# Moving the second expert bias from VectorE into the matmul of a gated attention and expert kernel

## The reference

```
x = x + tanh(g_xattn) * attention(layernorm(x), ctx, bias)     # 16 heads of 16, q/k/v with LoRA terms
x = x + tanh(g_ffn)   * ffn(layernorm(x))

def ffn(x):                       # 16384 tokens, E = 8 experts, H = I = 256
    idx = argmax(softmax(x @ Wg + bg))
    h = gelu(x @ W1[e] + b1[e])
    y = h @ W2[e] + b2[e]         # b2 is E x 256
    return y of expert idx of each token
```

## Time and profile before

| what | value |
|---|---|
| median of 3 runs | 1362.39 us (1362.06 to 1363.53) |
| profiled execution | 1363.53 us |
| its span, first to last instruction | 1361.7 us |
| TensorE busy | 1318.7 us, 97% of the span |
| VectorE busy | 1094.0 us, 80% |
| GpSimd busy | 1039.8 us, 76% |
| ScalarE busy | 889.3 us, 65% |
| granted TensorE clock, mean | 0.982 of 2.4 GHz |
| moved by DMA | 265.05 MB, mean 195 GB/s |

### The profile page before, as it was taken

How to read it: one execution, slowest core, us unless ns; L and a number is a source line. 1 busy time by engine, 2 the same in 40 slices (tenths; PEclk the granted TensorE clock), 3 DMA queues, 4 the chain that set the end, 5 groups by cost and what they waited for, 6 DMA issues and landing times.

```text
span 1361.7 us, 43106 instructions
## 1 busy us (share of the span) xinstructions
PE 1318.7 (97%) x13172; PEld 1137.3 (84%) x13172; DVE 1094.0 (80%) x2484; ACT 889.3 (65%) x1912; POOL 1039.8 (76%) x1186
## 2 busy tenths in 40 slices
PE   8999999999999999999999999999996599999997
PEld 6888888888888888888888888888885488888886
DVE  4898899899989898998998999989897355555555
ACT  3777777777777777777777777777775233333332
POOL 3778888888888888888888888888887254555445
PEclk7999999999999999999999999999999699999999
DMA  7656666666666666666666666666651598889984
GB/s 223 189 158 181 172 193 186 174 185 193 172 180 191 182 173 180 196 176 177 190 187 172 189 189 174 179 191 184 171 165 45 175 279 280 285 282 280 284 272 132
DMA packets 350200, 265.05 MB, mean 195 GB/s; under 512 B 17673, under 2 KB 313022, under 8 KB 350016
## 3 DMA queue, kind: packets, MB, share of 16 engines
q1 hardware_dynamic: 336656, 228.89, 59.4%
q0 software_dynamic: 12960, 34.63, 6.8%
q10 hardware_dynamic: 528, 0.84, 0.2%
HBM read 227.17 MB, written 38.94 MB: 195 GB/s over the span
## 4 chain that ended last, share of the span: by engine, by line
PE 92%; DVE 3%; issue 1%; DMA 1%; ACT 1%; POOL 1%; SPq 0%; POOLq 0%; DVEq 0%; ACTq 0%
PE bank L481 17%; PE bank L490 16%; PE bank L466 10%; PE bank L631 9%; PE bank L644 9%; PE bank L520 9%; PE bank L570 8%; PE bank L535 4%; PE bank L620 2%; PE bank L581 2%; PE bank L592 2%; PE bank L595 2%; PE bank L511 1%; DVE sc L820 1%; DVE negmax L826 1%
## 5 line engine op out<-in xcount | busy, mean ns | idle before, releaser
L378 POOL TENSOR_TENSOR sc<-sc,negmax 128x1024 f32<-128x1024 f32 x256 | 482.6, 1899 | 49.6 <-DVE negmax L826 45.7
L820 DVE TENSOR_TENSOR sc<-bank,sc 128x512 f32<-128x512 f32 x512 | 328.5, 683 | 44.6 <-PE bank L466 44.6
L826 DVE TENSOR_REDUCE negmax<-sc 128x8 f32<-128x1024 f32 x256 | 312.4, 1220 | 16.9
L694 ACT ACTIVATE PT<-bank 128x512 f32<-128x512 f32 x512 | 279.3, 606 | 0.2
L481 PE MATMUL bank<-cst,sc 128*128 128x128 f32 x2048 | 273.1, 276 | 0.0
L435 POOL DMA_INDIRECT out<-og,ids x142 | 139.8, 984 | 151.9 <-issue 130.8
L481 PEld LDWEIGHTS bank<-cst,sc 128*128 128x128 f32 x2048 | 226.1, 141 | 25.7 <-issue 25.5
L708 ACT COPY OT<-bank 128x512 f32<-128x512 f32 x128 | 75.0, 586 | 151.6 <-PE bank L520 151.6
L421 POOL DMA_INDIRECT rows_dram<-x2n,slot_i x128 | 138.6, 1083 | 29.5 <-issue 26.2
L466 PE MATMUL bank<-KT,QT 32*128 32x256 f32 x2048 | 146.6, 400 | 2.3 <-issue 1.8
L985 DVE SCALAR_TENSOR_TENSOR og<-bank,tg,sc 128x512 f32<-128x512 f32 x71 | 53.3, 751 | 109.7 <-PE bank L644 77.3
(11 more groups left out here) (114 smaller groups left out, 2186.2 us busy)
## 6 DMA issues: line engine op xcount, KB each, us to landing
sc<-in_bias SPq DMA_DIRECT2D x256, 512.0 KB
xg<-rows_dram SPq DMA_DIRECT2D x71, 272.0 KB
w_sb<-in_w SPq DMA_DIRECT2D x71, 257.0 KB
sc<-in_w SPq DMA_DIRECT2D x71, 256.0 KB
x_sb<-in_x SPq DMA_DIRECT2D x128, 128.0 KB, 2.1
ctx_sb<-in_ctx_in SPq DMA_DIRECT2D x128, 128.0 KB, 4.9
rows_dram<-vacant SPq DMA_DIRECT2D x9, 272.0 KB, 5.6
out<-og,ids POOLq DMA_INDIRECT x142
```

Source lines behind the costliest of these rows:

```text
L378: nc.gpsimd.tensor_tensor(s, s, m, ALU.add).then_inc(sub_ok, 1)
L694: nc.scalar.activation(PT[:, t.slot(2), 512 * q:512 * q + 512], b_t[q % 2][:], ACT.Exp).then_inc(pt_ready, 1)
L820: nc.vector.tensor_tensor(s, b_s[q][:], s, ALU.add).then_inc(s_used, 1)
L826: nc.vector.tensor_reduce(negmax[:, t.slot(2), 8 * h:8 * h + 8], sc[:, t.slot(4), 1024 * h:1024 * h + 1024].rearrange("p (h k) -> p h k", ...
```

## The change

The bias b2 is now added on TensorE. At the start VectorE splits b2 (8 x 256 float32) into three bf16 parts whose sum is b2; they are written to a small tensor in DRAM. In the expert stage SyncE loads the three rows of a tile's expert into partitions 0 to 2 of `b2_sb` (four slots, the other partitions are zero), as a third DMA beside the weights, and Y begins in each half with a matmul of `top3` (ones in partitions 0 to 2, zero elsewhere) and these rows. VectorE's L975, L1005 and L1007 go, as does the broadcast of b2. TILES becomes 72, and the writes of vacant rows are no longer spread over the stage: all eight are issued in the steps 0 to 7 that are written out, and the loads of rows in the loop wait for all of them.

```diff
-TILES = 71
+TILES = 72
+        b2_dram = nc.dram_tensor("b2_dram", (EXPERTS, 3, HID), BF16, kind="Internal").ap()
-        FLOOP = (1, TILES // FU)
+        FLOOP = (1, TILES // FU - 1)
-        TAIL_AT, TAIL_BY = 0, 5
 # SyncE, step 2 of the attention stage
-                    sp.dma_start(b2_all[:].rearrange("p e h -> p (e h)"), b2.rearrange("(a e) h -> a (e h)", a=1)
-                                 .partition_broadcast(P)).then_inc(b2_in, 16)
+                    sp.wait_ge(s_b2, 4)
+                    sp.dma_start(b2_dram, b2_parts[:]).then_inc(b2_out, 16)
 # SyncE, set-up loads
+            load(b2_all[:], b2, s_set)
 # SyncE, expert stage
+            sp.wait_ge(b2_out, 16)
             def fstep(i, k):
-                if k == TAIL_BY:
-                    sp.wait_ge(tail_out, i * 16 + 16)
-                    sp.nop(nofuse=True)
                 t = tile(i, k, -3)
                 if t:
                     if t.reached(8):
                         sp.wait_ge(og_ok, t.n(1, -7))
+                        sp.nop(nofuse=True)
+                    if not isinstance(i, int):
+                        sp.wait_ge(tail_out, 16 * EXPERTS)
                         sp.nop(nofuse=True)
...
                     sp.dma_start(w2_sb[:, t.slot(4)], w2[e]).then_inc(w2_in[t.slot(4)], 16)
-                if k == TAIL_AT:
-                    first = sp.value_load(tail_i[0:1, bass.ds(i, 1)], min_val=0, max_val=DUMMY - FT)
+                    sp.dma_start(b2_sb[0:3, t.slot(4)], b2_dram[bass.ds(e, 1)].rearrange("e p h -> (e p) h")
+                                 ).then_inc(w2_in[t.slot(4)], 16)
+                if isinstance(i, int) and 0 <= k < EXPERTS:
+                    first = sp.value_load(tail_i[0:1, k:k + 1], min_val=0, max_val=DUMMY - FT)
                     sp.dma_start(rows_dram[bass.ds(first, FT), :].rearrange("(p a) r -> p (a r)", p=P),
                                  vacant[:]).then_inc(tail_out, 16)
 # GpSimd, ahead of step 0
+            nc.gpsimd.memset(b2_sb[:], 0.0).then_inc(s_setg, 1)
 # TensorE, Y
-                    pe.wait_ge(w2_in[t.slot(4)], t.per(4, 16, 16))
+                    pe.wait_ge(w2_in[t.slot(4)], t.per(4, 32, 32))
                     for a in range(HALVES):
                         y_half = bank[6 + t.slot(2)][:, HID * a:HID * a + HID]
+                        mm(y_half, top3[:], b2_sb[:, t.slot(4), :], start=True, stop=False)
                         for c in range(KC):
                             ins = mm(y_half, hT[:, t.slot(2), c, a * P:a * P + P],
-                                     w2_sb[:, t.slot(4), c * HID:c * HID + HID], start=(c == 0), stop=(c == KC - 1))
+                                     w2_sb[:, t.slot(4), c * HID:c * HID + HID], start=False, stop=(c == KC - 1))
 # VectorE, set-up
+                nc.vector.memset(top3[:], 0.0).then_inc(s_set3, 1)
+                dve.wait_ge(s_set3, 1)
+                nc.vector.memset(top3[0:3, :], 1.0).then_inc(s_set3, 1)
+                nc.vector.tensor_copy(b2_parts[:, 0, :], b2_all[:]).then_inc(s_b2, 1)
+            def split_b2():
+                dve.wait_ge(s_b2, 1)
+                nc.vector.tensor_tensor(b2_rest[:], b2_all[:], b2_parts[:, 0, :], ALU.subtract).then_inc(s_b2, 1)
+                dve.wait_ge(s_b2, 2)
+                nc.vector.tensor_copy(b2_parts[:, 1, :], b2_rest[:]).then_inc(s_b2, 1)
+                dve.wait_ge(s_b2, 3)
+                nc.vector.tensor_tensor(b2_parts[:, 2, :], b2_rest[:], b2_parts[:, 1, :], ALU.subtract).then_inc(s_b2, 1)
 # VectorE, expert stage
-            dve.wait_ge(b2_in, 16)
-            nc.vector.tensor_scalar(b2_all[:], b2_all[:], tg[:, 1:2], None, ALU.mult).then_inc(b2_ok, 1)
-                    e = dve.value_load(tile_e[0:1, bass.ds(t.n(), 1)], min_val=0, max_val=EXPERTS - 1)
-                    dve.wait_ge(x2g_ok, t.n(HALVES, HALVES))
-                    nc.vector.tensor_tensor(x2g[:, t.slot(2)], x2g[:, t.slot(2)],
-                                            b2_all[:, bass.ds(e, 1), :].broadcast_to([P, HALVES, HID]), ALU.add
-                                            ).then_inc(x2b_ok, 1)
```

More of the change, by code:

```diff
@@ L129, in flamingo_block @@
         bv_all = sb("bv_all", [P, HID])
+        top3 = sb("top3", [P, P], BF16)
         bg_all = sb("bg_all", [P, EXPERTS])
@@ L189, in flamingo_block @@
         w1_sb = sb("w1_sb", [P, 4, KC * HID + KC])
-        b2_all = sb("b2_all", [P, EXPERTS, HID])
+        b2_sb = sb("b2_sb", [P, 4, HID], BF16)
+        b2_all, b2_rest = sb("b2_all", [EXPERTS, HID]), sb("b2_rest", [EXPERTS, HID])
+        b2_parts = sb("b2_parts", [EXPERTS, 3, HID], BF16)
         og = sb("og", [P, 2, HALVES, HID])
@@ L207, in flamingo_block @@
         s_cst, s_id, s_b, s_g, s_set, s_warm = (sem(t) for t in ("s_cst", "s_id", "s_b", "s_g", "s_set", "s_warm"))
-        s_bv, b2_in, b2_ok = sem("s_bv"), sem("b2_in"), sem("b2_ok")
+        s_bv, s_b2, b2_out = sem("s_bv"), sem("s_b2"), sem("b2_out")
         vacant_ok, vacant_out, tail_out = sem("vacant_ok"), sem("vacant_out"), sem("tail_out")
         s_setp, s_setd, s_seta, s_setg = sem("s_setp"), sem("s_setd"), sem("s_seta"), sem("s_setg")
-        s_setb, s_setr, s_ones = sem("s_setb"), sem("s_setr"), sem("s_ones")
+        s_set3, s_setb, s_setr, s_ones = sem("s_set3"), sem("s_setb"), sem("s_setr"), sem("s_ones")
         x_in = [sem(f"x_in{i}") for i in range(8)]
@@ L237, in flamingo_block @@
         w2_in = [sem(f"w2_in{i}") for i in range(4)]
-        ids_ok, inv_ok, x2g_ok, x2b_ok = (sem(t) for t in ("ids_ok", "inv_ok", "x2g_ok", "x2b_ok"))
+        ids_ok, inv_ok, x2g_ok = sem("ids_ok"), sem("inv_ok"), sem("x2g_ok")
         xg_in = [sem(f"xg_in{i}") for i in range(8)]
@@ L242, in flamingo_block @@
         og_out = [sem(f"og_out{i}") for i in range(2)]
-        SETUP_DMAS = 3
+        SETUP_DMAS = 4
         FIRST_DMAS = 2
@@ L364, in _ @@
             run_steps(sp, FFIRST, FLAST, FU, FLOOP, fstep)
-            for n, q in enumerate(og_out):
-                sp.wait_ge(q, 16 * HALVES * len(range(n, TILES, 2)))
+            for q in og_out:
+                sp.wait_ge(q, 16 * HALVES * TILES // 2)
         @block.gpsimd
@@ L934, in _ @@
             set_up_routing()
+            split_b2()
             run_steps(dve, 0, LAST, U, LOOP, step, {dve.engine: 0})
@@ L972, in _ @@
                                     ALU.min).then_inc(tab_ok, 1)
-            dve.wait_ge(b2_in, 16)
-            nc.vector.tensor_scalar(b2_all[:], b2_all[:], tg[:, 1:2], None, ALU.mult).then_inc(b2_ok, 1)
-            dve.wait_ge(tab_ok, 1)
             def fstep(i, k):
@@ L983, in fstep @@
                         dve.wait_ge(og_out[t.slot(2)], t.per(2, 16 * HALVES))
-                    dve.wait_ge(x2b_ok, t.n(1, 1))
+                    dve.wait_ge(x2g_ok, t.n(HALVES, HALVES))
                     nc.vector.scalar_tensor_tensor(out=og[:, t.slot(2)].rearrange("p a h -> p (a h)"),
@@ L1002, in fstep @@
                                                 ALU.subtract, ALU.mult).then_inc(x2g_ok, 1)
-                    if not t.reached(1):
-                        dve.wait_ge(b2_ok, 1)
-                    e = dve.value_load(tile_e[0:1, bass.ds(t.n(), 1)], min_val=0, max_val=EXPERTS - 1)
-                    dve.wait_ge(x2g_ok, t.n(HALVES, HALVES))
-                    nc.vector.tensor_tensor(x2g[:, t.slot(2)], x2g[:, t.slot(2)],
-                                            b2_all[:, bass.ds(e, 1), :].broadcast_to([P, HALVES, HID]), ALU.add
-                                            ).then_inc(x2b_ok, 1)
             run_steps(dve, FFIRST, FLAST, FU, FLOOP, fstep)
```

## The result

The change makes the kernel slower: a median of 1393.0 us (1392.3 to 1395.1) against 1362.5, a ratio of 1.0226 with a 95% interval of 1.0208 to 1.0243. The forecast was 1386.2 us with a range up to 1390.5, so the sign was right and the size too small: +30.5 us where +23.8 was forecast. The profiled execution took 1390.15 us (span 1388.2), 2.9 us under the median; it reached its first tile some 3 us earlier than that of before. The stage of the tiles is what is read from it.

A forecast was written before the change was run, and what follows sets the result against it. TensorE was taken to bound the kernel; 1363.5 + 19.6 (bf16 matmuls 15.8, tile 3.9) + 4.2 (wait) = 1387.3 us for a like execution, 1.1 above the median, so the forecast median was 1386.2 us, range 1381 to 1390.5.

The forecast's parts named there:

- What bounds: Expert stage: TensorE has no gap, so anything added there is paid in full and work taken from VectorE gains nothing.
- Rival E: Expert stage: transfers set the pace, the new matmuls hide and the kernel isn't slower, 1361.8 us; chance 0.03.
- Two more matmuls: Each half of Y in the expert stage: one bf16 matmul at 0.109 us, together 15.8 us.
- Rivals C and D: bf16 matmuls: C, 0.193 or 0.216 us each, 1398 to 1402 us, chance 0.10; D, bare weight loads, 1414 us, chance 0.01.
- The 72nd tile: TensorE's loop in the expert stage takes one more whole tile whatever it holds: +3.9 us.
- SyncE's queue, the pace: Expert stage's start: steps with a vacant write take 4.34 us against TensorE's 4.11, hidden by the queue's lead: 0.
- SyncE's queue, the wait: After the last vacant write: TensorE stands still once at T(11) and H(10), +4.2 us (3.3 to 5.2).
- Rival A: Wait for the vacant writes costs nothing, as writes or loads land sooner: 1382.0 us; chance 0.17.
- The clock: TensorE's granted clock after the stall: a fall to half was counted only in rival B, at +2.0 us.
- main case: TensorE's +19.6 us and one stall of +4.2 us: median 1386.2 us, own range 1385 to 1388; chance 0.52.
- rival B: The stall also costs the clock, +2.0 us, 1388.2 us, or is longer through traffic, to 1389.5 us; chance 0.15.
- What hides: VectorE's lost bias addition, splitting b2, fills, the dropped broadcast and the kernel's end: counted 0, at most -0.8 us.

The follow-up runs named there:

- b2_act_nobf16: Changed kernel with vacant writes one in eight tiles, bias loads issued by ScalarE, and no bf16 matmuls (b2 isn't added): 1366.9 us, ratio 1.0042.
- before72: The kernel before with 72 tiles instead of 71 and nothing else changed: 1367.4 us, ratio 1.0036.
- before_front: The kernel before with all eight vacant writes in SyncE's steps 0 to 7, waited for ahead of row loads in the loop: 1369.0 us, ratio 1.0062.
- late_wait: Changed kernel with SyncE's written-out steps going on to 15, so row loads wait for vacant writes only from tile 19: 1387.5 us, ratio 1.0173.
- act_tails: late_wait with the eight vacant writes issued by ScalarE instead of SyncE, in the same steps: 1382.5 us, ratio 1.0145.
- late_nob2: late_wait without the per-tile load of biases (zeros are added in place of b2): 1382.3 us, ratio 1.0149.
- warm: Changed kernel with eight spare f32 passes on TensorE ahead of the wait for the rows of tile 11: 1391.8 us, ratio 1.0220.
- before_warm: The kernel before with 28 spare f32 passes on TensorE between the tile table and the first rows: 1362.7 us, ratio 1.0007.

## Why the prediction was right and wrong

- **What bounds.** Right. Each tile is TensorE's sum, before and after, and what left VectorE bought nothing: b2_act_nobf16, which has neither the addition of the bias nor the bf16 matmuls, took 1366.9 us against 1367.4 of before72, the same within their intervals. No view shows the transfers as the bound, not even at a share of 1.01. Rival E falls.
- **Two more matmuls.** Right: 0.113 us each for 0.109, 16.3 us for 15.8. The bytes per partition of the nearest pass were the right measure. Rivals C and D (exposed loads) fall.
- **The 72nd tile.** Right, 3.9 us by its period; before72 bears it out.
- **SyncE's queue, the pace.** This is the step that failed. The prediction put a step with all four issues at 4.34 us, by adding 0.52 to a step of 3.82 read where the queue waited for nothing, and concluded that "these delays hide behind the lead that the queue had, with 0.6 us left at the end". A step took 4.79 us. The third load was priced nearly right: the same step without it took 4.21 us (before_front), so it costs 0.58. The step of 3.82 was what was too short, by 0.4. It was read from rows to rows; from weights to weights the same step of before took 1077.94 to 1081.92, 3.98 us:

```profile
1081.92 0.33 SPq L357 DMA_DIRECT2D w_sb<-in_w  x1
```

In the change the weights follow the rows by 1.15 to 1.44 us where 1.1 was charged, already at tile 3, whose weights wait for no Y (1079.96 to 1081.29), and the write follows the load of biases by 1.29, where 1.61 - 0.52 = 1.09 was charged. From the first weights to those of tile 9 the queue took 40.37 us (1069.69 to 1110.06) for the 36.85 forecast, 3.5 us more. The lead was also 1.2 us smaller, since H of tile 1 began 7.13 us after the first weights' issue and not 8.31. Of these 4.7 us the lead of 0.6 took up its part, and 0.1 went since tile 9's weights reached H in 3.6 us and not 3.7. That leaves about the 3.9 us by which H of tile 9 came late (3.6 when counted from T to T), in place of 0. late_wait, act_tails and late_nob2 show that it was this and not the traffic. Why a weights issue stands 1.15 to 1.44 us behind the rows' in these steps no run shows.
- **SyncE's queue, the wait.** Right in place and mechanism: T(11) and then H(10), behind rows issued after the last write had landed. The write landed in 3.50 us, just under the lower bound of 3.7, and the stall without the clock was 3.6 us for 4.2, inside the 3.3 to 5.2. In before_front the write took 5.03 us, also inside the bounds of 3.7 to 5.6. The prediction's other figure for it, 2.6 us, rests on a fit that the Trainium skill, "DMA: Bandwidth & Descriptors", section "Anatomy of one DMA — SWDGE (gpsimd) path", gives for transfers issued by GpSimd. This write is SyncE's, and no run shows one that landed so soon. Rival A, a wait that costs nothing, falls.
- **The clock.** The main case left it out and gave it to rival B at 0.15. It fell, and cost 3.2 us in the profile where B had 2.0, since Y was slow as well as H. warm suggests that the net cost was nearer 1 than 3 us. No rule for the fall comes out of the runs: the clock held in before_front through waits of 1.5 and 1.7 us, and fell in the change after 2.1 us.
- **What hides.** Right, as far as the profiles tell: the end behind the last tile's T takes 17.4 us, 0.6 more than before, of which the bf16 matmuls of the last two Ys make 0.45.
- **The sum.** 16.3 + 3.9 + 3.6 + 3.6 + 3.2 = 30.6 against 30.5 measured. Forecast were 15.8 + 3.9 + 0 + 4.2 + 0. The missing 6.8 us are the pace's 3.6 and the clock's 3.2; the wait's 0.6 too much and the matmuls' 0.5 too little cancel. That the five terms meet the median to 0.1 us is in part luck: they are read from one profile that lies 2.9 us under it, and by its interval the difference is 28.3 to 33.1 us. The range ended at 1390.5, since it allowed for the wait and the clock together but held the pace at nothing, and in this profile all three came. (The chances as stated add up to 1.01.)

## What to carry to other kernels

Where one engine issues all transfers, its queue has a period of its own, and each small load adds its issue to it: add up what a step takes with its waits, in the busiest steps, and hold it against the bound engine's period before anything else; a lead lasts only until the difference, times the steps taken, has used it up. A transfer moved to the queue of an engine with time to spare (here ScalarE, busy for some 36 of 100 us) took its stalls away though the same bytes moved in the same steps. A load that seems free beside longer work (the third load at 4.12 us a tile) may have its price uncovered when that work is taken away (9 us at 3.89).

## What the runs showed of the hardware

- With the DMA engines at a share of 1.01 and 334 GB/s over 8 us (act_tails) no matmul waited for a load; the kernel before stood at 0.90 and 282 GB/s over 100 us. A write of 0.28 MB from SyncE landed in 3.50 us in the change and in 5.03 in before_front.
- On SyncE an issue stood 0.51 us behind the one before it, and 1.1 us or more where a register load came between; three loads, one write and their register loads took 4.79 us a step, and 4.21 without the third load.
- TensorE's granted clock fell to 0.50 after a stall in which it had worked 0.32 of 2 us, and in before_warm after waits of 2.0, 0.9 and 1.0 us between short bursts of work. It stayed at 1.00 in warm, with 1.7 us of spare passes in the wait, and in before_front, with 0.36 of 2 us of work.
- bf16 matmuls of 256 columns set between f32 passes cost 0.113 us each, with no charge for changing the kind of operand.
